# A graph network's first layer: the weighted neighbour sum as a dense product over pairs of nodes, in place of scatter-adds

## What is computed

```python
def L0_gnn(x, src, dst, edge_vals, w, b):          # cut to what matters
    h = x @ w
    deg = segment_sum(edge_vals, src, n); dinv = where(deg > 0, rsqrt(deg), 0)
    out = segment_sum(h[dst] * (dinv[src] * edge_vals * dinv[dst])[:, None], src, n)
    return relu(out + b)
x = x + L0_gnn(layernorm(x), src, dst, edge_weight, L0_gnn_w, L0_gnn_b)
x = x + L0_ffn(layernorm(x))                       # layers 1 to 3 follow
```

## Time and profile before

| what | us |
|---|---|
| median of 3 runs (lowest, highest) | 8010.51 (8003.66, 8014.09) |
| the profiled execution | 7996.99 |
| its span | 7995.0 |
| PE, DVE, ACT, POOL busy | 5968.8, 4801.9, 2966.1, 3435.1 |

### The profile page before, as it was taken

One profiled execution on the slowest core, in us unless ns is written; L12 is line 12 of the kernel. 1 busy time (PEld: TensorE's weight loads), 2 busy tenths in 40 slices (PEclk: granted clock), 3 DMA queues, 4 the chain that ended last, 5 costly groups with the idle time before them and its releaser, 6 DMA issues. The chain is left out here.

```text
span 7995.0 us, 122318 instructions
## 1 busy us (share of the span) xinstructions
PE 5968.8 (75%) x30884; PEld 4285.4 (54%) x30885; DVE 4801.9 (60%) x10565; ACT 2966.1 (37%) x7906; POOL 3435.1 (43%) x2953
## 2 busy tenths in 40 slices
PE   7377566666663668788887696788887599587898
PEld 5155444444442435555565384566665488366666
DVE  7588533333333455788887625899998511687333
ACT  0033344444442224455554231454544333233333
POOL 1100188888884013777775041777775022000000
PEclk9855688888886779899998798999998799798999
DMA  3055699999997028777776143777776233321000
GB/s 157 31 176 177 170 190 191 189 188 186 189 191 188 4 69 318 219 230 230 231 230 162 44 135 105 231 234 239 238 236 168 101 111 103 121 99 39 8 12 20
DMA packets 671115, 1231.15 MB, mean 154 GB/s; under 512 B 93515, under 2 KB 477309, under 8 KB 658692
## 3 DMA queue, kind: packets, MB, share of 16 engines
q0 software_dynamic: 276016, 679.29, 33.9%
q1 hardware_dynamic: 388148, 540.62, 21.6%
q10 hardware_dynamic: 6560, 6.55, 0.3%
HBM read 902.62 MB, written 323.50 MB: 153 GB/s over the span
## 5 line engine op out<-in xcount | busy, mean ns | idle before, releaser
L2262 POOL DMA_INDIRECT rows<-l_kv,index_staged x1708 | 1721.4, 1008 | 706.6 <-issue 499.4
L1289 POOL DMA_INDIRECT gcn_sums<-out,target x806 | 1308.2, 1623 | 283.8 <-issue 156.8
L2375 PE MATMUL sum<-messages,hot 128*128 128x260 f32 (+1 forms) x3416 | 953.2, 408 | 53.5 <-issue 24.5
L2351 PE MATMUL q<-queries,spread 128*128 x5136 | 712.3, 285 | 129.0 <-DVE rows L2512 82.3
L2321 ACT ACTIVATE messages<-rows,messages 128x64 f32<-128x64 f32 (+1 forms) x3392 | 774.4, 323 | 0.0
L1309 PE MATMUL g<-same,hot 128*128 128x128 f32 x1612 | 319.0, 374 | 522.2 <-DVEq L1367 481.0
L2375 PEld LDWEIGHTS sum<-messages,hot 128*128 128x128 f32 x3416 | 606.4, 195 | 156.6 <-issue 74.0
L2512 DVE TENSOR_TENSOR rows<-q,rows 128x512 f32<-128x512 f32 x854 | 572.3, 683 | 142.2 <-DMA rows<-l_kv,index_staged 141.2
L2351 PEld LDWEIGHTS q<-queries,spread 128*128 128x128 bf16 x5136 | 483.3, 101 | 322.1 <-issue 218.2
L1309 PEld LDWEIGHTS g<-same,hot 128*128 128x128 f32 x1612 | 290.5, 277 | 619.4 <-issue 567.9
L1360 DVE TENSOR_SCALAR before<-before 128x13 f32<-128x13 f32 x62 | 11.3, 182 | 891.2 <-DMA gcn_sums<-out,target 890.6
(11 more groups left out here) (543 smaller groups left out, 11802.1 us busy)
## 6 DMA issues: line engine op xcount, KB each, us to landing
window<-gcn_rows SPq DMA_DIRECT2D x806, 128.0 KB
edge_counts<-count_stage SPq DMA_DIRECT2D x21, 3800.0 KB
rel<-slot_rel SPq DMA_DIRECT2D x218, 256.0 KB
src_row<-in_src_row SPq DMA_DIRECT2D x62, 832.0 KB
counts<-edge_counts SPq DMA_DIRECT2D x8, 4800.0 KB
first_part<-in_L_ffn_first SPq DMA_DIRECT2D x32, 1030.0 KB
rows<-l_kv,index_staged POOLq DMA_INDIRECT x1708
edge_attr<-in_attr SPq DMA_DIRECT2D x124, 208.0 KB
```

The source lines that it names most:

```text
L1289: pool.indirect_dma_start(out=copies[m], out_offset=bass.IndirectOffsetOnAxis(ap=target[:, u, j:j + 1], axis=0), in_=out[:, u, j, :], in_o ...
L2262: pool.indirect_dma_start(out=rows[:, u * 2 + n, j, :], out_offset=None, in_=table, in_offset=bass.IndirectOffsetOnAxis(ap=staged[:, u, n ...
L2351: ins = pe.matmul(q_ps[g % QUERY_BANKS][:, r, :], spread[:, t[1] * 2 + n, g * RUN % U + r, :], qs[:, bass.ds(tile, 1), m, :], start=m == 0 ...
L2375: ins = pe.matmul(sum_ps[g % 2][:, 0:W], hot[:, n, j, :], messages[:, n, j, :, :].rearrange("p h d -> p (h d)"), start=r == 0, stop=r == R ...
```

## The change

The sum is computed as a product with a dense 3125 x 3125 matrix of edge weights, and that matrix is built beside the counts.

- Groups have 5 nodes instead of 4 (`PAIR_ROWS` = 125 keys instead of 100 columns); there are 97 windows instead of 108, in blocks of 3 instead of 5 (33 instead of 22).
- `edge_units` (was `count_units`) also brings the edge weights into lanes by unit: seven transposes in front, and one more set of 56 products (L538).
- `edge_matrices` (was `count_edges`): PSUM holds one window of counts and one of weights (four banks each). For each window POOL multiplies the bf16 key one-hot by the weights into f32 (`key_w`, 15x125 wide), ACT copies the bf16 lane one-hot to f32 (`lane_f`, 15x128 wide), and PE adds 15 f32 products `key_w` x `lane_f` in a second window. ACT copies that one, too, and SP stores it to `pair_weights` in DRAM.
- `edge_tables` loses the fourth column group, the self loops, and the tables for the scatter; POOL no longer fills tables with zeros.
- `dense_sum` (was `scatter_sum`): 25 steps of 125 source rows for each of three groups of result tiles (10, 10, 5) are 75 steps and 625 f32 products of 125 x 128 pair weights with 125 x 256 of `h`, summed in five PSUM banks. SP loads the pair weights six steps ahead. Ten products stand in each of the 62 batches of the edge network. DVE applies `dinv`, bias, ReLU and the residual when a bank is complete. There is no indirect DMA, no `same`, `hot`, `g` or `o`.
- `CopySums` is gone.

```diff
-        self.gcn_rows = nc.dram_tensor("gcn_rows", [NWIN, D], F32, kind="Internal").ap()
-        self.gcn_sums = [nc.dram_tensor(f"gcn_sums{m}", [NWIN, D], F32, kind="Internal").ap() for m in range(SUM_COPIES)]
+        self.gcn_rows = nc.dram_tensor("gcn_rows", [NPAD, D], F32, kind="Internal").ap()
...
-NODES_EACH = 4
-COUNT_COLS = NODES_EACH * TILES
+NODES_EACH = 5
+PAIR_ROWS = NODES_EACH * TILES
...
-BLOCK_WINDOWS = 5
+BLOCK_WINDOWS = 3
...
+                dve.wait_ge(weighed, 1)
+                for q, at, n in parts:
+                    ins = dve.tensor_copy(unit_w[:, at:at + n], key_ps[q][:, 0:n])
+                step(ins)
...
+                pe.wait_ge(weight_in, 16)
+                for r, c, m in spans:
+                    real = min(m, CHUNKS - c)
+                    pe.transpose(key_ps[r // 4][0:real, r % 4 * P:(r % 4 + 1) * P], by_lane[:, c:c + real], k.ident[:, :]
+                                 ).then_inc(turned, 1)
+                pe.wait_ge(weight_rows, R)
...
+                for q, at, n in parts:
+                    pe.wait_ge(keyed, q + 1)
+                    for r, c, m in spans:
+                        ins = pe.matmul(key_ps[q][:, 0:n], weight[0:m, r, :], chosen[0:m, r, at:at + n],
+                                        start=r == 0, stop=r == R - 1)
+                ins.then_inc(weighed, 1)
...
+        lane_f, key_w = ph.sb("lane_f", [P, 2, U, P]), ph.sb("key_w", [P, 2, U, C])
-        stage = ph.sb("count_stage", [P, 2, TILES, BLOCK_SLOTS * E])
+        count_stage = ph.sb("count_stage", [P, 2, TILES, BLOCK_SLOTS * E])
+        weight_stage = ph.sb("weight_stage", [P, 2, BLOCK_SLOTS * P])
+        count_ps, weight_ps = (ph.ps(n, [P, WINDOW_BANKS, 512]) for n in ("count_window", "weight_window"))
...
-                pool.memset(stage[:, :, :, :], 0.0).then_inc(made, 1)
+                pool.memset(count_stage[:, :, :, :], 0.0).then_inc(made, 1)
+                for w in range(WINDOWS):
+                    shape = [P, U, C]
+                    pool.wait_ge(keys_hot, w + 1)
+                    pool.tensor_tensor(key_w[:, w % 2, :, :], hot_key[:, w % 2, :, :],
+                                       unit_w[:, w * U:(w + 1) * U].unsqueeze(2).to_broadcast(shape), ALU.mult
+                                       ).then_inc(keys_weighed, 1)
...
+                    if w:
+                        pe.wait_ge(count_kept, w)
+                    begin(count_ps, P, C)
+                    if w:
+                        at = nc.snap(regs[U], min_val=0, max_val=(BLOCK_SLOTS - 1) * E)
+                        pe.matmul(counts[:, 0:C], k.ident[:, :], count_stage[:, last, :, bass.ds(at, E)].rearrange("p s e -> p e s"),
+                                  start=False, stop=False)
+                    pe.wait_ge(lanes_hot, w + 1)
+                    pe.wait_ge(keys_hot, w + 1)
                     for j in range(U):
                         at = nc.snap(regs[j], min_val=0, max_val=U * SLOT_COLS)
+                        pe.matmul(counts[:, bass.ds(at, C)], hot_lane[:, u, j, :], hot_key[:, u, j, :], start=False, stop=False)
+                    end(count_ps, P).then_inc(count_full, 1)
                     if w:
+                        pe.wait_ge(weight_kept, w)
+                    begin(weight_ps, C, P)
+                    if w:
+                        at = nc.snap(regs[U + 1], min_val=0, max_val=(BLOCK_SLOTS - 1) * P)
+                        pe.matmul(weights[0:C, 0:P], k.ident[0:C, 0:C], weight_stage[0:C, last, bass.ds(at, P)],
+                                  start=False, stop=False)
+                    pe.wait_ge(lanes_wide, w + 1)
+                    pe.wait_ge(keys_weighed, w + 1)
+                    for j in range(U):
+                        at = nc.snap(regs[j], min_val=0, max_val=U * SLOT_COLS)
+                        pe.matmul(weights[0:C, bass.ds(at, P)], key_w[:, u, j, :], lane_f[:, u, j, :], start=False, stop=False)
+                    end(weight_ps, C).then_inc(weight_full, 1)
...
+                def widen(w):
+                    act.wait_ge(lanes_hot, w + 1)
+                    act.activation(lane_f[:, w % 2, :, :], hot_lane[:, w % 2, :, :], ACT.Copy).then_inc(lanes_wide, 1)
...
+                    act.wait_ge(count_full, w + 1)
                     if w:
+                        act.wait_ge(count_kept, w)
+                    at = nc.snap(regs[0][j], min_val=0, max_val=(BLOCK_SLOTS - W) * E)
+                    out = count_stage[:, b % 2, :, bass.ds(at, W * E)].rearrange("p s (g e) -> p s g e", e=E)
+                    counted = count_ps[:, :, :].rearrange("p b (g c) -> p (b g) c", c=SLOT_COLS)[:, :, 0:C]
+                    act.activation(out, counted.rearrange("p g (e s) -> p s g e", s=TILES), ACT.Copy).then_inc(count_kept, 1)
+                    if w + 1 < WINDOWS:
+                        widen(w + 1)
+                    act.wait_ge(weight_full, w + 1)
+                    if w:
+                        act.wait_ge(weight_kept, w)
+                    at = nc.snap(regs[1][j], min_val=0, max_val=(BLOCK_SLOTS - W) * P)
+                    act.activation(weight_stage[0:C, b % 2, bass.ds(at, W * P)],
+                                   weight_ps[0:C, :, :].rearrange("p b c -> p (b c)"), ACT.Copy).then_inc(weight_kept, 1)
...
+        weight_parts = ph.sb("weight_parts", [P, 3, CHUNKS], BF16)
+        tile_w = ph.sb("tile_w", [P, 2, 3, TILES, BATCH], BF16)
...
-                clear_rows(pool, k.gcn_sums + [k.gcn_rows[NPAD:NWIN, :]], zeros, cleared)
...
+SUM_BANKS = 5
+SUM_TILES = 2 * SUM_BANKS
+KEYS = PAIR_ROWS // NODES_EACH
+STEP_NODES = KEYS * NODES_EACH
+STEPS_EACH = NODES // STEP_NODES
+SUM_STEPS = [(t, min(SUM_TILES, TILES - t), n) for t in range(0, TILES, SUM_TILES) for n in range(STEPS_EACH)]
+PRODUCTS = [(s, j) for s, (t, width, n) in enumerate(SUM_STEPS) for j in range(width)]
+PER_BATCH = len(PRODUCTS) // BATCHES
+SHARES = (1, 3, 5, 7, PER_BATCH)
...
+                def load(s):
+                    t, width, n = SUM_STEPS[s]
+                    if s >= RING:
+                        sp.wait_ge(used, s - RING + 1)
+                    for e in range(E):
+                        sp.dma_start(pairs[e * KEYS:(e + 1) * KEYS, s % RING, 0:width, :],
+                                     weights[e, t:t + width, n * KEYS:(n + 1) * KEYS, :].rearrange("t g c -> g t c")
+                                     ).then_inc(pairs_in[s % RING], 16)
...
+                    for s in range(2, len(SUM_STEPS)):
+                        if b == (last_of[s - RING] + 1 if s >= RING else 0):
+                            load(s)
...
+                def multiply(first, last):
+                    for s, j in PRODUCTS[first:last]:
+                        t, width, n = SUM_STEPS[s]
+                        if j == 0:
+                            pe.wait_ge(pairs_in[s % RING], (s // RING + 1) * (16 * E))
+                        if n == 0 and t and j % 2 == 0:
+                            pe.wait_ge(emptied, (t - SUM_TILES + j) // 2 + 1)
+                        ins = pe.matmul(sum_ps[j // 2][:, j % 2, :], pairs[0:S, s % RING, j, :], h[0:S, n, :],
+                                        start=n == 0 and j % 2 == 0,
+                                        stop=n == STEPS_EACH - 1 and (j % 2 == 1 or j == width - 1))
+                        if j == width - 1:
+                            ins.then_inc(used, 1)
+                        elif n == STEPS_EACH - 1 and j % 2:
+                            ins.then_inc(summed, 1)
+
+                for b in range(BATCHES):
+                    at = b * PER_BATCH
+                    multiply(at, at + SHARES[0])
+                    if b == 0:
+                        pe.wait_ge(mlp.w_in, 16 * (4 + JOBS))
+                    for q in range(4):
+                        mlp.hidden(pe, b, b % 2, q // 2, q % 2)
+                        multiply(at + SHARES[q], at + SHARES[q + 1])
+                    mlp.result(pe, b)
+                multiply(BATCHES * PER_BATCH, len(PRODUCTS))
...
+                    for m in range(width):
+                        node_tile = t + 2 * b + m
+                        ins = dve.scalar_tensor_tensor(total[:, n % 2, m, :], sum_ps[b][:, m, :],
+                                                       k.dinv[:, node_tile:node_tile + 1], bias[:, :], ALU.mult, ALU.add)
+                    ins.then_inc(emptied, 1)
+                    dve.wait_ge(emptied, n + 1)
+                    at = slice(t + 2 * b, t + 2 * b + width)
+                    dve.scalar_tensor_tensor(k.x[:, at, :], total[:, n % 2, 0:width, :], 0.0, k.x[:, at, :], ALU.max, ALU.add
+                                             ).then_inc(scaled, 1)
...
-    scatter_sum(k, table, copies)
...
+    dense_sum(k, table)
...
-            routed(k, xn, xT, a["L0_ffn_gW"], 4, logits, summed=True)
+            routed(k, xn, xT, a["L0_ffn_gW"], 4, logits)
```

(43 more changed lines are left out.)

434 lines of the change are left out of this document (121 added, 313 removed).

## The result

| | before | after |
|---|---|---|
| median (lowest to highest), 4 runs each | 8012.3 (8003.66 to 8018.06) | 7900.69 (7877.84 to 7906.4) |
| profiled execution, span | 7996.99, 7995.0 | 7899.83, 7898.3 |
| ratio of the times, 95% interval | | 0.9856 (0.9835 to 0.9878) |

A forecast was written before the change was run, and what follows sets the result against it. It took the scatter sum's 806 indirect DMAs on POOL as the main bound, then windows and `routed`. Terms -901 + 451 - 30 + 5 + 6 - 83 = -552 from 7996.99 gave 7445, stated as 7450 us, range 7310 to 7620.

The forecast's parts named there:

- The windows, 480.4 to 931: Window stage: 97 windows at 9.5 us plus 9 for the last window and stores, a cost of 451 us.
- the register load: Ahead of each window PE's sequencer loads registers, 1.1 to 3.8 us; 1.0 exposed at full clock, none at half.
- Stores: 5.9 MB a block: Window stage: storing a block of three windows takes 19 us of about 28 at 309 GB/s, and hides.
- The rest of the window's sum: Per window: PE 8.65 us at full clock, 10.8 at half; f32 passes 0.12 or 0.22; POOL's multiply 4.24; DVE's one-hots 4.3.
- The port pair: Windows: DVE and POOL exclude each other, at least 8.5 us a window; as rival deciding alone, 8.6 to 8.7, 7370, 20%.
- The clock: PE's clock in the windows, unreadable: port-pair rival has 1.00 (7370, 20%), half-clock rival 0.50, 10.8 us a window (7576, 20%).
- The dense sum: Sum stage, 1601.7 to 701 us: 62 batches at 10.9, 18 ahead for loading `h`, 7 behind; a gain of 901.
- The degree tables: Degree tables: a quarter off DVE's `tile_w` and PE's columns, between 10 and 40 us, taken as 30 off.
- `edge_units` and the zero-fill: Ahead of the windows: `edge_units` +5 us (0 to +20) for 56 more f32 passes; zero-fill +6, or -3 side by side.
- `routed`: `routed` without the copies: as the like phase's 45.6 us instead of 128.7, 83 off (between 70 and 88).
- a window of over 15.3 us: Rival, slower than before: windows over 15.3 us, needing POOL's multiply at 11 us; 8075 at 16 us a window; 3%.
- taking turns: Rival, windows: POOL, PE and DVE work in turn, 13.1 us a window, 340 us more, 7790; 7%.

The follow-up runs named there:

- rows of 17: The kernel before with its rows of 16 unit places put 17 integers apart, still 16 registers a load: 8241.9 us, window stage 712.7.
- both mended: The changed kernel with unit-place rows 20 integers apart and pair weights stored from 128 partitions: 7413.51 us, ratio 0.9256, window stage 849.7.
- 128 rows of weights: The changed kernel with pair weights kept in DRAM with 128 rows and stored from 128 partitions instead of 125: 7837.84 us, window stage 1274.1.
- rows of 20 alone: The changed kernel with rows of unit places 20 integers apart instead of 17, still 17 registers loaded: 7710.36 us, window stage 1135.3.

## Why the prediction was wrong

- **The windows, 480.4 to 931: wrong, and by this the whole.** The step that failed is the one on the register load: "Ahead of each window PE's sequencer loads its registers, at 1.1 us and up to 3.8 ... I take 1.0 exposed at full clock and none at half." 4.5 were exposed (434 over 97). PE's own work was within the forecast: 9.05 us busy a window (878 over 97), between the 7.65 and 10.8 that the sum gives without the load; 9.05 and 4.5 are 13.5 of the 13.7. I had read the load's price from the earlier trace rows and taken it over, though the change lengthened the row it reads from 64 to 68 bytes. The kernel before with rows of 17 shows that this alone turns 1.10 into 3.80 and, beside a store, 3.5 into 9.5 to 11. A load of 1.36 cost nothing: PE didn't stand idle after any of the ten.
- **"Stores: 5.9 MB a block ... 19 us of about 28; they hide": wrong.** They took 34, 12 for the counts and 22 for the weights, of the 40 us that three windows lasted, and more than the 28 of my forecast. I worked with bytes and one rate, and left the number of rows out, though it had gone from 128 to 125 in the lines of the change. The slow loads hid this; without them it stopped the stage at 1135.
- **The rest of the window's sum was right or too dear.** With both mended the stage is 849.7 where I had 931, and the kernel 7413 where I had 7450; that the two are so near is partly luck, the stage 81 cheaper and the dense sum 47 dearer. POOL's multiply took 3.31 and not 4.24. It reads one operand in bf16 and one as a broadcast column, where the one in the earlier trace rows reads two wide ones in f32; which of this made it faster no run shows. The f32 passes took 0.11 us each at full clock and 0.20 near half, for my 0.12 and 0.22 (rows below).
- **The port pair** excludes as the earlier trace rows say: DVE's `hot_key` takes 2.10, and 5.22 the one time that it met POOL's multiply (its first, of 5.15). With both mended 57 of the 97 `hot_lane` met one, and each ended 2.01 after POOL had, whatever its start. It was no bound: DVE idled 857 us. With both mended windows start every 8.5 us, but that isn't the 8.5 of my sum, which had 4.24 for POOL: the pair now needs 4.3 + 3.3 = 7.6, and DVE still stands idle 346 us in all ahead of `hot_lane`. First `hot_key` in the changed kernel, then `hot_lane` with both mended:

```profile
L594 DVE TENSOR_TENSOR hot_key<-lanes_b,unit_key x97: 2099/2105/5225, 372.3 to 1646.4; 128x1875 bf16<-128x1875 bf16 x97
L594 DVE TENSOR_TENSOR hot_lane<-lanes_b,unit_lane x97: 2151/3077/4772, 370.9 to 1184.0; 128x1920 bf16<-128x1920 bf16 x97
```

- **The clock**, which I couldn't read, was neither rival's: 0.70 with the waits, 0.85 without. In the changed kernel a window's 30 passes took 3.44 at a clock of 1.00 and 5.90 at 0.57:

```profile
907.06 5.90 PE L640 MATMUL weight_window<-lane_f,key_w 128*125 128x128 f32 x30
916.04 3.44 PE L640 MATMUL weight_window<-lane_f,key_w 128*125 128x128 f32 x30
```

- **The dense sum: right in its mechanism and its period**, 10.88 for 10.9. The four hidden groups of a batch were 1.96, 2.21 and 1.96 apart, for my 2.13. The start was mis-sized, by 47 us. The first product came after 36 us where I had 18: SP takes 18.6 to issue `h`, and the first step's pair weights are there 17 later. Then PE stood 9 ahead of the first hidden group, whose weights SP issues behind the pair weights. The gap ahead of the second batch, 20 us over the period, is the features' wait behind 20 more transfers of pair weights. All are in this view of SP's and PE's first instructions:

```profile
1749.39 18.55 SPq L1253 DMA_DIRECT2D h_by_step<-gcn_rows  x5
1767.98 18.75 SPq L1248 DMA_DIRECT2D pairs<-pair_weights  x10
1785.16 1.19 PE L1297 MATMUL sum<-h_by_step,pairs 125*128 125x256 f32 x2 [39.33 <-DMA pairs<-pair_weights]
1793.19 25.89 SPq L1248 DMA_DIRECT2D pairs<-pair_weights  x20
1795.54 1.75 PE L765 MATMUL edge_h<-edge_attr,edge_w 64*128 64x416 f32 x4 [9.20 <-issue]
1819.13 1.94 SPq L750 DMA_DIRECT2D edge_attr<-in_attr  x2
1826.00 1.75 PE L765 MATMUL edge_h<-edge_attr,edge_w 64*128 64x416 f32 x4 [17.89 <-DMA edge_attr<-in_attr]
```

- **The degree tables** gave 20 and not 30; DVE's `tile_w` fell by the 0.18 of 0.88 that I had put at 0.22. `edge_units` and the zero-fill were dearer in the forecast than in the run; DVE's and POOL's fills ran beside each other:

```profile
353.43 9.67 POOL L574 MEMSET count_stage<- 128x11500 f32 x1
355.95 9.87 DVE L585 MEMSET weight_stage<- 128x11776 f32 x1
```

- **`routed`**: right, 45.7 for 46. It gave 79.7 and not 83, as I had read 3 us of the next phase into the 128.7 of before.
- **The chances.** I had given 3% to a window of over 15.3 us, by POOL's multiply. The window came to 13.7 by another way, near the time of my "taking turns" (13.1, 7790; added up right, 7800), but not by it: PE waited for POOL only once, 2.3 us. I had given 96% to faster, and that came true with a fifth of the gain, so it says little for the reasoning. No rival of mine had the register load or the width of a store in it.

What stays open: why a load from such a row costs three times as much; no view shows how the row is read. Why loads are slower beside a store is open too. What the remaining loads beside a store of counts (4.3 us) would give if they read elsewhere was not tried.

## What to carry to other kernels

When a change alters a shape, price again every instruction that reads or writes it, down to register loads and single stores, by where a row begins and how many rows there are, not by bytes. An instruction that costs nothing in the profile of before may do so by the good luck of its layout. And an edit that gives less than its reason promises may have met the next bound: mend the two together before judging either.

## What the runs showed of the hardware that I had not expected

- A load of PE's registers from SBUF takes 1.10 us for 16 and 1.36 for 17 if the row begins at a multiple of 16 bytes from the table's start, and 3.80 and 4.04 if not. Where it meets a store over all engines it takes up to 3.8 and 4.6, and up to 11.2 and 14.5 if not aligned (the kernel before, rows and store mended, the kernel before with rows of 17, the changed kernel).
- A store of 125 rows of 23.5 KB goes at 136 GB/s (the changed kernel), one of 128 such rows at 428 (with 128 rows of weights).
- The same 6301 instructions of PE were 132 us shorter in busy time when it waited 341 us less, at a granted clock of 0.85 for 0.70 (rows and store mended); with rows of 20 alone it waited some 200 us less and was no shorter.
